# Attention with an FFN in parallel: batch loops written out, V read from the transposed input, a PSUM bank moved from the exponent scores to the maximum scores

## The reference

```python
xn  = layernorm(x)                                   # over the 256 features
Q, K, V = xn @ W_q.T, xn @ W_k.T, xn @ W_v.T         # 16 heads of 16 features
Qr, Kr = rope(Q), rope(K)
scores = einsum('bhqd,bhkd->bhqk', Qr, Kr) * 16 ** -0.5
scores = where(key after query, smallest float, scores)
heads  = einsum('bhqk,bhkd->bhqd', softmax(scores), V)
attn   = heads.reshape(b, t, d) @ W_o.T
ffn    = fake_quant_fp8(xn) @ fake_quant_fp8(weight).T + bias   # one scale for the whole tensor
out    = x + attn + ffn
```

## Time and profile before

| | |
|---|---|
| median of 3 runs | 481.42 us |
| span of the profiled execution, first to last instruction | 479.7 us |
| TensorE matmuls busy | 413.3 us (86%) |
| VectorE busy | 352.8 us (74%) |
| ScalarE busy | 278.5 us (58%) |
| GpSimd busy | 274.8 us (57%) |
| mean granted TensorE clock | 0.918 |

### The profile page before, as it was taken

The page is one execution under the profiler, slowest core; times in us unless marked ns, Lnnn a source line. Parts: engine busy times, 40 slices in busy tenths (PEclk is TensorE's granted clock), DMA queues, the critical chain, the costliest instruction groups (busy, mean ns, idle before and its releaser), DMA issues.

```text
span 479.7 us, 10238 instructions
## 1 busy us (share of the span) xinstructions
PE 413.3 (86%) x2819; PEld 224.7 (47%) x2819; DVE 352.8 (74%) x1340; ACT 278.5 (58%) x500; POOL 274.8 (57%) x278
## 2 busy tenths in 40 slices
PE   1771667899999999999999969999999999998976
PEld 1431411264346455645564535545555544554544
DVE  3779799868779887988798827978897868852041
ACT  2734731047765776577657742587468665666840
POOL 2204576436747963796389631985498427327560
PEclk9995555599999999999999986999999999999997
DMA  7728458211482339323923391145714671020021
GB/s 249 254 76 223 107 178 198 66 46 44 153 202 93 100 104 199 135 86 117 243 92 108 109 227 48 44 135 152 189 56 135 165 196 39 5 86 6 1 87 45
DMA packets 39789, 57.55 MB, mean 120 GB/s; under 512 B 5280, under 2 KB 31264, under 8 KB 39712
## 3 DMA queue, kind: packets, MB, share of 16 engines
q1 hardware_dynamic: 39744, 57.03, 42.0%
HBM read 35.78 MB, written 17.04 MB: 110 GB/s over the span
## 4 chain that ended last, share of the span: by engine, by line
PE 44%; POOL 18%; DMA 11%; issue 11%; ACT 7%; DVE 4%; SPq 3%; ACTq 0%; POOLq 0%; DVEq 0%
PE o_ps L935 9%; PE st_ps L854 9%; DMA qk_parts<-parts 8%; PE s_ps L871 7%; PE m_ps L907 5%; PE m_ps L810 4%; POOL parts L268 4%; PE m_ps L882 4%; ACT prob L734 3%; POOL prob L440 3%; POOL rot L264 3%; POOL rot L258 2%; POOL xq L470 2%; SPq L370 2%; POOL qv L466 2%
## 5 line engine op out<-in xcount | busy, mean ns | idle before, releaser
L599 DVE CUSTOM_DVE_ANT_0 scratch<-s_ps,causal 128x512 bf16<-128x512 f32 (+3 forms) x512 | 224.2, 487 | 64.4 <-PE s_ps L871 53.7
L734 ACT ACTIVATE prob<-st_ps 128x512 f32<-128x512 f32 x320 | 175.6, 600 | 104.4 <-PE st_ps L854 104.2
L440 POOL TENSOR_SCALAR_AFFINE_SELECT prob<-prob 128x512 f32<-128x512 f32 (+1 forms) x160 | 86.8, 546 | 141.8 <-ACT prob L734 141.0
L871 PE MATMUL s_ps<-k_st,q_st 96*128 96x512 bf16 (+3 forms) x512 | 132.4, 322 | 21.8 <-DVE rowmax L599 18.6
L854 PE MATMUL st_ps<-q_st,k_st 98*128 98x128 bf16 (+3 forms) x512 | 121.1, 303 | 1.0 <-ACT prob L734 0.9
L935 PE MATMUL o_ps<-prob,v_sb 128*17 128x512 f32 (+3 forms) x1024 | 87.8, 439 | 6.0 <-ACT heads L749 5.2
L871 PEld LDWEIGHTS s_ps<-k_st,q_st 96*128 96x128 bf16 x512 | 47.1, 99 | 73.3 <-DVE rowmax L599 48.2
L854 PEld LDWEIGHTS st_ps<-q_st,k_st 98*128 98x128 bf16 x512 | 43.5, 98 | 64.5 <-ACT prob L734 26.8
L599 DVE DVE_READ_ACCUMULATOR2_ANT rowmax<- 128x1 f32 x512 | 42.3, 83 | 0.0
L935 PEld LDWEIGHTS o_ps<-prob,v_sb 128*17 128x17 f32 x1024 | 20.4, 96 | 44.1 <-issue 35.6
L907 PE MATMUL m_ps<-wo_sb,attnT 128*128 128x256 f32 x128 | 35.1, 398 | 1.0 <-ACT attnT L755 0.5
(11 more groups left out here) (96 smaller groups left out, 496.7 us busy)
## 6 DMA issues: line engine op xcount, KB each, us to landing
qk_parts<-parts SPq DMA_DIRECT2D x16, 768.0 KB, 3.8
q_st<-qk_parts SPq DMA_DIRECT2D x32, 192.0 KB, 3.6
k_st<-qk_parts SPq DMA_DIRECT2D x32, 192.0 KB, 3.7
q_st<-x_dram SPq DMA_DIRECT2D x8, 512.0 KB, 5.4
q_st<-qk_parts SPq DMA_DIRECT2D x32, 128.0 KB, 3.7
k_st<-qk_parts SPq DMA_DIRECT2D x32, 128.0 KB, 3.7
xn_v<-xnT SPq DMA_DIRECT2D x8, 512.0 KB, 3.7
x_res<-x_dram SPq DMA_DIRECT2D x8, 512.0 KB, 3.5
```

The source lines that it names most:

```text
L440: eng.affine_select(out=ap, in_=ap, compare_op=ALU.is_ge, fill=0.0, base=0, pattern=pat, channel_multiplier=-1).then_inc(masked, 1)
L599: eng.tensor_tensor_reduce(scratch[:, f % 2, col:col + w], s_ps[f % 2][:, col:col + w], causal[:, T - w:T], 1.0, NEG, ALU.add, ALU.max, ro ...
L734: eng.activation(prob[u][:, half * T:(half + 1) * T], st_ps[ST_BANK[2 * s + half]][:, :], ACT.Exp, scale=SCALE).then_inc(exp_done, 1)
L871: mm = eng.matmul(s_ps[f % 2][:, col:col + (qb + 1) * P], q_st[0:ROWS, 1 - par, h, qb * P:(qb + 1) * P], k_st[0:ROWS, 1 - par, h, 0:(qb + ...
```

## The change

All loops over batches are written out: `each_batch` goes through its eight batches in plain code on each engine, and `run` does so with iterations -1 to 8. `project_v` reads its operand from `xnT`, and `xn_v`, its two DMAs and its semaphore are gone. The exponent scores have two banks and the maximum scores three: half `i` uses bank `i % 2` and waits for the exponent of half `i - 2`; bank `f` of the maxima is counted across batches modulo 3 and waits for the reduction of bank `f - 3`. In the first part the fourth bank for turning is `s_ps[2]` in place of `st_ps[2]`.

```diff
-ST_BANK = [i % 3 for i in range(HALVES - 1)] + [1]
+ST_BANK = [i % 2 for i in range(HALVES)]
 def each_batch(eng, step, between):
-    for n in range(4):
+    for n in range(NB):
         step(n, n % 2)
         between(n)
-    with eng.Fori(2, NB // 2) as i:
-        for p in range(2):
-            step(2 * i + p, p)
-        xn_v = sb("xn_v", [P, NC, T])
-        scratch = sb("scratch", [P, 2, T], BF16)
+        scratch = sb("scratch", [P, 3, T], BF16)
-        st_ps = [pb(f"st_ps{i}", [P, T]) for i in range(3)]
-        s_ps = [pb(f"s_ps{i}", [P, T]) for i in range(2)]
+        st_ps = [pb(f"st_ps{i}", [P, T]) for i in range(2)]
+        s_ps = [pb(f"s_ps{i}", [P, T]) for i in range(3)]
-        turn_ps = [[st_ps[0], st_ps[1]], [st_ps[2], o_ps]]
+        turn_ps = [[st_ps[0], st_ps[1]], [s_ps[2], o_ps]]
-        LOOP = (2, 6)
-        def run(eng, iteration):
-            every = {1, 2, 3, 4}
-            iteration(-1, 1, {2}, set())
...
-            with eng.Fori(0, (LOOP[1] - LOOP[0]) // 2) as i:
-                iteration(2 * i + LOOP[0], 0, every, every)
-                iteration(2 * i + LOOP[0] + 1, 1, every, every)
...
+        FIRST = {1: 0, 2: -1, 3: 0, 4: 1}
+        LAST = {1: NB - 3, 2: NB - 2, 3: NB - 1, 4: NB}
+        def stages_of(b):
+            return {st for st in FIRST if FIRST[st] <= b <= LAST[st]}
+        def run(iteration):
+            for b in range(-1, NB + 1):
+                iteration(b, b % 2, stages_of(b), stages_of(b - 1))
-                if 3 in stages and 2 in stages:
-                    eng.wait_ge(full["v"], 2 * (b + 1))
-                    eng.dma_start(xn_v[:, :, :], xnT[:, :, bass.ds((b + 1) * T, T)]).then_inc(xnv_in, 16)
-            eng.wait_ge(xnT_copied, 2 * NB)
-            eng.dma_start(xn_v[:, :, :], xnT[:, :, 0:T]).then_inc(xnv_in, 16)
+                    at = (BANKS * (b + 1) + f) % 3
-                        eng.tensor_tensor_reduce(scratch[:, f % 2, col:col + w], s_ps[f % 2][:, col:col + w],
+                        eng.tensor_tensor_reduce(scratch[:, at, col:col + w], s_ps[at][:, col:col + w],
-                    wait_past(eng, max_done, ITEMS * n + (ITEMS_UP_TO[f - 2] if f >= 2 else ITEMS_UP_TO[f - 2] - ITEMS))
+                    wait_past(eng, max_done, ITEMS * n + (ITEMS_UP_TO[f - 3] if f >= 3 else ITEMS_UP_TO[f - 3] - ITEMS))
+                    bank = s_ps[(BANKS * n + f) % 3]
-                    if i == 0:
-                        eng.wait_ge(xnv_in, 16 * (b + 1))
-                                            xn_v[:, c, (2 * i + t) * P:(2 * i + t + 1) * P],
+                                            xnT[:, c, b * T + (2 * i + t) * P:b * T + (2 * i + t + 1) * P],
```

More of the change, by code:

```diff
@@ L162, in attention_ffn_block @@
         shared = {(kind, k): m_ps[bank] for (kind, k), bank in SHARED_BANK.items()}
-        turn_ps = [[st_ps[0], st_ps[1]], [st_ps[2], o_ps]]
-        first_ps = m_ps + s_ps
+        turn_ps = [[st_ps[0], st_ps[1]], [s_ps[2], o_ps]]
+        first_ps = m_ps + s_ps[0:2]
         qk_dram = nc.dram_tensor("qk_parts", [2, 2, 3, 2, J, H, T], BF16, kind="Internal").ap()
@@ L270, in attention_ffn_block @@
         block = ctx.enter_context(nc.Block())
-        LOOP = (2, 6)
-        def run(eng, iteration):
-            every = {1, 2, 3, 4}
-            iteration(-1, 1, {2}, set())
-            iteration(0, 0, {1, 2, 3}, {1, 2})
-            iteration(1, 1, every, {1, 2, 3})
-            with eng.Fori(0, (LOOP[1] - LOOP[0]) // 2) as i:
-                iteration(2 * i + LOOP[0], 0, every, every)
-                iteration(2 * i + LOOP[0] + 1, 1, every, every)
-            iteration(6, 0, {2, 3, 4}, every)
-            iteration(7, 1, {3, 4}, {2, 3, 4})
-            iteration(8, 0, {4}, {3, 4})
+        FIRST = {1: 0, 2: -1, 3: 0, 4: 1}
[5 more added lines that the diff above has]
+                iteration(b, b % 2, stages_of(b), stages_of(b - 1))
         @block.sync
@@ L388, in _ @@
             key_stacks(1, 1, False)
-            eng.wait_ge(xnT_copied, 2 * NB)
-            eng.dma_start(xn_v[:, :, :], xnT[:, :, 0:T]).then_inc(xnv_in, 16)
-            run(eng, iteration)
+            run(iteration)
             eng.wait_ge(y_out, 16 * NB)
@@ L866, in scores_for_max @@
                         eng.wait_ge(stack_in[g], 16 * 6 * (n + 1))
-                    wait_past(eng, max_done, ITEMS * n + (ITEMS_UP_TO[f - 2] if f >= 2 else ITEMS_UP_TO[f - 2] - ITEMS))
+                    wait_past(eng, max_done, ITEMS * n + (ITEMS_UP_TO[f - 3] if f >= 3 else ITEMS_UP_TO[f - 3] - ITEMS))
+                    bank = s_ps[(BANKS * n + f) % 3]
                     for i, qb, col in MAX_BANKS[m]:
                         h = 2 * pair + i
-                        mm = eng.matmul(s_ps[f % 2][:, col:col + (qb + 1) * P],
+                        mm = eng.matmul(bank[:, col:col + (qb + 1) * P],
                                         q_st[0:ROWS, 1 - par, h, qb * P:(qb + 1) * P],
```

1 line of the change is left out of this document (removed).

## The result

The changed kernel takes 469.54 us, median of 4 runs (468.62 to 470.29), beside 481.75 (481.33 to 482.16) for the kernel before: a ratio of 0.9741, 95% interval 0.9723 to 0.9760. Forecast were 469.1 us and 463.5 to 474.5. Its profiled execution took 468.62 us with a span of 466.9; what lies around the span is 1.7 us, as before.

A forecast was written before the change was run, and what follows sets the result against it. TensorE, busy for 86% of the span, was taken as the main limit. Terms 8.9 + 0.2 + 2.6 + 0.9 + 0 + 1.7 - 2.0 = 12.3 us off 481.4 gave 469.1 us, range 463.5 to 474.5.

The forecast's parts named there:

- The branch back: Iteration 4, at the loop's branch back: written out it runs at the normal pace, saving 8.9 us (8.2 to 9.2).
- The first part: Short loops of the first part: registers and branches saved by writing out, 0.2 us gain (0 to 0.6).
- Iteration -1: Third maximum bank removes VectorE's 12 waits on TensorE (2.4 us) plus 0.2 of lead: 2.6 us gain (0 to 3.2).
- Iterations 0 and 1: Waits removed before slot 13 of iteration 0 gain 0.9 us (0 to 2.5); later ones only lengthen the k_st wait.
- The full iterations: Each full iteration gains 0.25 us and pays 0.23 for the exponent bank: nothing, within -0.4 to +0.4.
- Iteration 6: TensorE's waits for VectorE go, 2.5 us, but uncovered exponent waits take 0.8: 1.7 us gain (0.6 to 2.4).
- Iteration 7: With two exponent banks second halves wait longer for ScalarE's exponents: 2.0 us loss (0.5 to 3.0).
- Straight code stalls: Rival: one VectorE stall of 3.70 us stays at the passage from iteration 3 to 4, 472.8 us; chance 0.09.
- written-out code does not do what it says: Rival: stalls stay at the same place for another reason than the branch, gain 3.4, 478.0 us; chance 0.04.
- The third bank brings nothing outside: Rival: shift rows hold iteration -1 and exponents iteration 6, so gain is 7.9, 473.5 us; chance 0.12.
- The bank helps the full iterations too: Rival: third maximum bank gains 0.8 us in each of five iterations, 465.1 us; chance 0.17.
- The tie to ScalarE: Rival: two exponent banks cost 2.0 us in every iteration with attention, 16.0 in all, 483.1 us; chance 0.06.

The follow-up runs named there:

- the first experiment: All batch loops written out against the kernel before, with three exponent banks, two maximum banks and xn_v kept: 473.99 us, ratio 0.9828.
- the third: The changed kernel with two maximum banks in place of three, its exponent banks still two, the freed bank only for turning: 476.72 us, ratio 0.9884.

## Why the prediction was right, step by step

**The branch back.** Predicted 8.9, measured 8.98 in the table and 8.5 us of median with writing out alone. The step took the neighbouring iteration as the model of the one to come, and for iteration 4 of the kernel after that was right. The reason was right as well: only VectorE's branch cost anything by itself. But the 8.98 us are not all this term's. With the loops written out and nothing else, iterations 2 to 5 take 190.66 us in place of 198.18, a gain of 7.5, since iteration 3 grew by 0.85 and iteration 4 stayed 0.46 above 47.19. (With VectorE alone written out they take 189.43.) The other 1.6 us, down to the 189.06 of the kernel after, came with the change of banks.

**The first part.** Predicted 0.2 us of gain; measured 1.04 us of loss, which nothing ties to the edit. The same written-out first part ended at 57.7 to 59.0 us in the five kernels that have it besides the one after, and the same looped one at 57.06, 59.09 and 59.21 in the three that have that. A term of 0.2 us can't be seen under a spread of 2.

**Iteration -1.** Predicted 2.6 of at most 3.2, measured 3.36, outside the bound by little. The 12 waits, 2.4 us, went as forecast. Most of the rest is something that I had not counted: the reductions themselves became shorter. (The 0.2 us of TensorE's lead that I counted can't be told from what remains.) VectorE's groups of 512 and 128 columns in this stretch (count, busy us, mean ns), of before and after:

```profile
L599 DVE CUSTOM_DVE_ANT_0 scratch<-s_ps,causal 128x512 bf16<-128x512 f32 x16 | 11.0, 688 | 3.5 <-PE s_ps L871 3.5
...
L599 DVE CUSTOM_DVE_ANT_0 scratch<-s_ps,causal 128x128 bf16<-128x128 f32 x16 | 4.6, 288 | 1.1 <-PE s_ps L871 1.1
```

```profile
L587 DVE CUSTOM_DVE_ANT_0 scratch<-s_ps,causal 128x512 bf16<-128x512 f32 x16 | 10.9, 679 | 2.3 <-PE s_ps L860 2.3
...
L587 DVE CUSTOM_DVE_ANT_0 scratch<-s_ps,causal 128x128 bf16<-128x128 f32 x15 | 4.2, 278 | 0.0
```

The means fall by 9 and 10 ns, that of the read-out from 81 to 76. Over 64 items of about 12 ns (reduction and read-out) that is 0.8 us, which with 2.4 makes up 3.2 of the 3.36. What would be late next, the shift rows, was named rightly: SyncE issued their read at 87.20 in the kernel after, and with the transfers kept it cost 0.2 us of waiting and 0.43 in all, less than the 1.1 I had given.

**Iterations 0 and 1.** Predicted 0.9 of gain in iteration 0 and nothing in 1; measured -0.47 and +0.66, together +0.19. This term is the one that went wrong, and the earlier trace rows had one reason in them: what opens iteration 1 is the chain from GpSimd's `low` through DRAM to `k_st`. In the kernel after (chain that ended last):

```profile
124.64 2.12 POOL parts L263
...
126.77 3.71 DMA qk_parts<-parts
...
131.32 3.13 DMA k_st<-qk_parts
134.45 0.05 issue
134.49 0.39 PE s_ps L860
```

Measured from the first exponent scores of iteration 0, `low` starts after 34.86 us (124.64 - 89.78), and before it was 34.69 (126.79 - 92.10): GpSimd gained nothing from the third bank. The first maximum scores of iteration 1 came at 44.71 us from there, 44.33 before. What TensorE gained in iteration 0 against the kernel before it then spent on the landing. I had said that waits removed behind slot 13 go this way; those before it did too. The other reason is a price that the sum left out, that of the exponent bank here. By the experiments the third maximum bank gives 1.41 us in iteration 0 and loses 0.46 of them in iteration 1, so 0.95 in all, about the 0.9 forecast; giving up the exponent bank takes 0.69 (0.77 less 0.08). One pair of traces can't tell much less than that: iterations 0 and 1 together take 91.49 us in the kernel before, and 91.97 and 92.21 with the same code in the two kernels that only divide the main loop.

**The full iterations.** Predicted a gain and a loss that cancel, measured 0.14 us over three of them. The experiment with two and two banks shows that the cancelling is real: without the third maximum bank iterations 3 and 5 take 47.86 and 48.15 us, with it 47.20 and 47.19. Over iterations 2 to 5 the maximum bank gives 2.3 us, 0.57 in each where I had 0.25, and the exponent bank takes 0.9, the 0.23 in each of the forecast. So beside the written-out kernels the swap gains 1.4 to 1.6 us; beside the kernel before hardly anything, because there iterations 3 and 5 stood at 47.19 and 47.18 already. GpSimd is in the way now, as the step said: in the iteration from 276.2 to 323.4 TensorE's waits for `rowmax` are gone, and in their place is

```profile
PE o_ps L922 <- POOL prob L427: 0.8, 1, 0.8
```

beside 0.7 us for ScalarE's `heads`.

**Iteration 6.** Predicted 1.7, measured 1.68, and the mechanism is shown from both sides: the `rowmax` waits gone, the exponent waits uncovered (6.0 us by weight loads), and 43.11 us again with two maximum banks. Half 6, the first of slot 3, whose start I had compared in the earlier trace rows with the end of the exponent two before, does stand behind it now: it starts at 377.20, after a wait of 0.28 us for ScalarE.

**Iteration 7.** Predicted a loss of 2.0, measured 2.06, and it accrues pair by pair as the step said. At slot 3 of the kernel after:

```profile
417.56 1.12 ACT L722 ACTIVATE prob<-st_ps 128x512 f32<-128x512 f32 x2
418.24 0.11 PEld L842 LDWEIGHTS st_ps<-q_st,k_st 98*128 98x128 bf16 x2 [0.87 <-ACT prob L722]
418.25 0.88 PE L842 MATMUL st_ps<-q_st,k_st 98*128 98x128 bf16 x4 [0.59 <-ACT prob L722]
418.53 0.63 ACT L737 COPY heads<-o_ps 128x512 f32<-128x512 f32 x1
418.73 0.11 PEld L842 LDWEIGHTS st_ps<-q_st,k_st 98*128 98x128 bf16 x2 [0.38 <-ACT prob L722]
```

The four matmuls are the two halves of the slot. The first, at 418.25, stands behind the exponent two before, and so does the second: its weights come at 418.73, when the second exponent of the pair has ended. In the kernel before the second half started with the first exponent's end, at 431.15. Counted from the first matmul of the iteration the second half starts at 6.26 us before and 6.76 after, the 0.49 us forecast. What stays of such delays at the start of later halves, worked out from both timelines (half, us before, us after, difference):

```
half  8    9.30    9.79   0.49   (behind slot 3)
half 12   12.98   13.48   0.50   (slot 5: its delay of 1.2 us is covered)
half 18   18.20   19.19   0.99   (slot 8)
half 22   20.88   22.35   1.47   (slot 10)
half 26   23.50   25.29   1.79   (slot 12)
half 39   32.92   34.98   2.06   (slot 17 adds 0.27)
```

Of the four pairs named three paid in full and one was covered; two of those with less to lose paid 0.3 each. With five banks the same halves 8, 18 and 39 start at 8.44, 17.30 and 31.75 us: the kernel before had been losing 0.86 us at slot 3 already.

**The tail.** Predicted 0, and 1.9 us shorter. It was not the edit: its PEclk was 0.81 in the kernel before,

```profile
460.90:479.70 18.80, 11.36 (x48) 7.72 (x48) 5.38 (x14) 1.94 (x5) 7.01 (x3) 0.81 0.25 82
```

and 1.00 in the one after. In the executions with loops on VectorE or on the others it was 19.8 as well, without any of the changes to banks; in that with five banks 21.70. So the span flatters the change by 1.9 us and the first part takes off 1.0. The two errors are within 1 us of cancelling each other, and the sum of 12.3 came out at 12.8 in the spans and 12.2 in the medians for that reason too.

**The rivals.** "Straight code stalls" and "written-out code does not do what it says" fell with the first experiment. "The third bank brings nothing outside" fell with the third: 3.36 us in iteration -1 and 1.67 in iteration 6, and against the kernel before only iterations 0 and 1 bear it out. "The bank helps the full iterations too" is true in part: 0.3 to 1.0 us in each beside two exponent banks, and 1.6 in all against the kernel that is only written out, where the rival had 4; against the kernel before it doesn't show, as writing out had cost about as much. The tie to ScalarE costs 2.06 us in iteration 7 and 0.77 in iteration 0, nothing like 2 us in each.

## What to carry to other kernels

Price a removed stall by the neighbouring pass that doesn't have it, and ask of each engine apart whether its branch back costs anything: here VectorE's loop cost 6.3 us alone and 9.0 beside four others, and those four alone cost nothing. The DMA view shows which loops fetch at their branch and which don't. Buffers should follow the work: the bank moved from exponents to maxima pays where both chains run or where the maxima alone do, costs where they don't, and lending the idle banks out in the last iteration took back more than the move had cost. A gain ahead of a landing that comes through another engine (here GpSimd, DRAM, `k_st`) turns into a longer wait; measure both from the same event before counting it.

## What the runs showed that I had not expected

- A second stall of VectorE one slot behind the branch, in straight code: 3.70 and 2.03 us, with a transfer of instructions of its own. It never shows without the branch.
- Four engines branch back without any instructions being moved.
- With a third bank the reductions themselves are shorter, by 5 to 10 ns of 81 to 688. VectorE's busy time over the whole span falls from 352.8 to 350.1 us; with two banks each it is 352.0. Why a reduction with its input long ready should be shorter was not followed.
- TensorE's clock falls to half in stretches that differ between kernels and executions: behind the branch (from 287.6 us for 6.8 us in the kernel with the loop on VectorE alone, after a wait of TensorE of 1.62 us for `rowmax`), in the tail, and once in iteration 1, right behind a wait of 1.95 us for `k_st` (in the kernel after the same wait was 1.63 us and the clock stayed at 1.00). Whole runs of the kernel after had mean clocks of 0.938, 0.938, 0.938 and 0.930, and 469.85 us or less in the first three, 470.29 in the last. A 2 us difference in one stretch of one profile can be this alone.
